# Path attention's preparation: raw products two slabs apart, and root and reciprocal replaced by a power on GpSimd

## The chip, the core and the metric

The kernel runs on one core of a Trainium2 chip. The time is device microseconds (us) of one execution of the whole program. Before the change it is 2883.48 us, the median of three runs (2875.68 to 2893.51). The core's engines work side by side and are tied together by semaphores only: PE (TensorE, matrix products), DVE (VectorE), ACT (ScalarE), POOL (GpSimd) and SP, which issues the DMAs.

## The reference

The program is a six-step model block (cross attention, linear attention, a top-2 mixture of experts, a filtered cross attention, path attention, an expert-choice layer), all in fp32 on x of 16 x 64 x 256. The change touches the first half of the fifth step. Cut to what matters:

```
q, k, v = (h @ m.T for m in (q_w, k_w, v_w))            # h: layer norm of x
w_raw = h @ w1.T @ w2.T                                 # low rank, 32
w_raw = silu(sum(shift(w_raw, i) * conv_w[:, i] for i in range(3)))
Ah, Bh = even and odd halves of w_raw                   # per head and direction, 16 channels each
Wdir = Ah * cos(theta) + Bh * sin(theta)
Wdir = Wdir * rsqrt(sum(Wdir * Wdir, -1) + 1e-06)       # this line is what changes
beta = 2 * sigmoid(h @ bt_w.T + bt_b)
```

## The kernel before, in words

`path_attention` (from L1678) has two blocks with a barrier between them. The first, the **preparation**, makes q, k, v, the directions w and the scaled directions wb for all 1024 tokens. The second, from L1967, solves the triangular systems and the attention batch by batch; it is untouched but for its line numbers. Nothing of the second block starts before every engine has ended the first.

The 512 direction channels are four groups g = 0 to 3 of 128 rows; a group's tile is 128 x 1024 (all tokens), and PSUM takes it in halves of 512 columns. PSUM has 8 banks of 128 x 512: the raw products (and later v) use banks 0 to 3, the norms banks 4 and 5, the projections banks 6 and 7.

- **Raw products** of group g (PE, L1811): four 32 x 512 products, two kinds (a = 0, 1) by two halves. ACT copies each twice out of PSUM (L1854, L1856, the second scaled by the last tap of the convolution) and counts `r_sb`.
- **Slabs** (PE, L1791): twelve projections of 128 output rows, four each for beta, k and q. Each is two halves of two accumulated products; ACT evicts each half (L1864 with the sigmoid, L1866). A slab's half can start only when ACT has evicted the same half of the slab before.
- `convolve(g)` (DVE, L1896, L1898): four instructions. `silu(g)` (ACT, L1839): one over both kinds. `rotate(g)` (DVE, L1904 to L1907): four products and sums, the last of them the square.
- `norms(g)` (PE, L1803): two products with a 0/1 matrix, which add the squares over 16 rows. `roots(g)` (ACT, L1844): Sqrt of the two halves, with 1e-6 as bias.
- `normalise(g)` (DVE): `reciprocal` (L1911), then w times it (L1912), then wb (L1915).
- **Values** (PE, L1820): 64 small products, v for every batch; ACT evicts four banks (L1876).

Each engine runs its own list in the order in which the code issues it; a waiting instruction holds up all that are behind it on its engine. PE: raws(g), three slabs, and norms(g-2) from g = 2 on; then the values, norms(2) and norms(3). ACT follows the same order with silu(g-1) and roots(g-2). DVE: convolve(0), then convolve(g), rotate(g-1) and, from g = 2 on, normalise(g-2); rotate(3), normalise(2), normalise(3). POOL only makes masks in this block (L1734 to L1767). SP loads the weights and then the slabs, the next one as soon as the last but one is in PSUM.

ACT loads a table before a function that the loaded one does not hold: here Sigmoid, Silu and Sqrt each need another, Copy none.

One other place matters for the prediction: in the fourth step POOL already raises a column to the power of -1 (L1267, `tk_total`, one column) and multiplies one (L1271).

Of the kernel before, what the change touches and what calls it, by code (L numbers as in the profile page):

```python
# [13 lines left out]
P = 128  # L14
# [1658 lines left out]
def path_attention(core):  # L1673
# [11 lines left out]
    with ExitStack() as stack:  # L1685
# [14 lines left out]
        with ExitStack() as inner:  # L1700
# [6 lines left out]
            conv, bb = isb("conv", [P, 2, G, 3]), isb("beta_bias", [P, G])  # L1707
            raw, ab = isb("raw", [P, 2, 2, NT]), isb("ab", [P, G, 2, NT])
            blocks = isb("blocks", [P, P])
            eps = isb("eps", [P, 1])  # L1710
            w_loaded, slab_loaded = sem("weights_loaded"), [sem(f"slab_loaded{i}") for i in range(2)]
            step, p_ps, p_sb = sem("step"), sem("proj_in_psum"), sem("proj_ready")
            l_ps, l_sb, r_ps, r_sb = sem("low_in_psum"), sem("low_ready"), sem("raw_in_psum"), sem("raw_ready")
            c_done, s_done, sq_done, n_ps, n_sb, n_used, b_done = (sem(n) for n in ("conv_done", "silu_done", "square_done",
                "norm_in_psum", "norm_ready", "w_ready", "wb_ready"))
            v_ps, v_sb = sem("v_in_psum"), sem("v_ready")
            block = inner.enter_context(nc.Block())
            SLABS = [("beta", wb), ("k", k), ("q", q)]
# [10 lines left out]
            @block.gpsimd  # L1729
            def _(pool):  # L1730
                core.zero_last_stage(pool)
                c = Chain(chained, pool)
                g = nc.gpsimd
                select = lambda o, pattern, base, cm, fill, op=ALU.is_ge: c.link(g.affine_select(  # L1734
                    out=o, in_=o, compare_op=op, fill=fill, base=base, pattern=pattern, channel_multiplier=cm))
                c.step(g.memset(eps[:], 1e-6))
                upper, mincl = mq_mask[:, 0], mq_mask[:, 1]
                for o, value in ((upper, 1.0), (mincl, -1.0), (below[:], 1.0), (causal[:], 0.0), (ident_c[:], 0.0),
                                 (blocks[:], 1.0)):
                    c.link(g.memset(o, value))  # L1740
                halves = (slice(0, T), slice(T, P))
                for rows in halves:
                    select(mq_mask[rows, 0], [[1, T]], -1, -1, 0.0)
                    select(mq_mask[rows, 1], [[1, T]], 0, -1, 0.0)
                    select(below[rows, :], [[-1, T]], -1, 1, 0.0)
                    select(causal[rows, :], [[-1, T]], 0, 1, -1e30)
                    select(ident_c[rows, :], [[-1, T]], 0, 1, 1.0, ALU.not_equal)

                def same_blocks(s, o):

                    c.link(g.memset(o[:], 1.0))
                    for rows in halves:
                        select(o[rows], [[-s, T // s], [0, s]], 0, 1, 0.0)
                        select(o[rows], [[s, T // s], [0, s]], s - 1, -1, 0.0)

                same_blocks(2, same)
                c.link(g.tensor_tensor(firstT[:], same[:], upper, ALU.mult))
                c.link(g.tensor_scalar(firstT[:], firstT[:], -1.0, None, ALU.mult))
                for n, s in enumerate(LEVELS):
                    m = levelT[:, n, :]  # L1760
                    same_blocks(2 * s, m)
                    c.link(g.tensor_tensor(m, m, same[:], ALU.subtract))
                    c.link(g.tensor_tensor(same[:], m, same[:], ALU.add))
                    c.link(g.tensor_tensor(m, m, upper, ALU.mult))
                select(blocks[:], [[-16, P // 16], [0, 16]], 0, 1, 0.0)
                select(blocks[:], [[16, P // 16], [0, 16]], 15, -1, 0.0)
                g.memset(same[:], 0.0).then_inc(masks, 1)  # L1767

            @block.tensor
            def _(pe):  # L1770
                ln.tensor(pe)
                pe.wait_ge(w_loaded, 6 * 16)
                for n in range(2):
                    pe.wait_ge(ln.xnT_ready, 2 * n + 2)
                    for c in range(KD):
                        mm = nc.tensor.matmul(ps[0:32, 4 + n, :], w1[:, c, :], ln.xnT[:, c, n * 512:(n + 1) * 512],
                                              start=(c == 0), stop=(c == KD - 1))
                    mm.then_inc(l_ps, 1)
                pe.wait_ge(l_sb, 2)
                made = 0  # L1780

                def slabs(count):

                    nonlocal made
                    for m in range(made, made + count):
                        pe.wait_ge(slab_loaded[m % 2], 16 * (m // 2 + 1))
                        for n in range(2):
                            if m:
                                pe.wait_ge(p_sb, 2 * (m - 1) + n + 1)
                            for c in range(KD):  # L1790
                                mm = nc.tensor.matmul(ps[:, 6 + n, :], wsm[:, m % 2, c, :],  # L1791
                                                      ln.xnT[:, c, n * 512:(n + 1) * 512], start=(c == 0), stop=(c == KD - 1))
                            mm.then_inc(p_ps, 1)
                    made += count

                def norms(g):

                    pe.wait_ge(masks, 1)
                    pe.wait_ge(sq_done, g + 1)
                    for n in range(2):  # L1800
                        if g:
                            pe.wait_ge(n_sb, 2 * g + n - 1)
                        nc.tensor.matmul(ps[:, 4 + n, :], blocks[:], ab[:, g, 1, n * 512:(n + 1) * 512],  # L1803
                                         start=True, stop=True).then_inc(n_ps, 1)

                for g in range(G):
                    if g:
                        pe.wait_ge(r_sb, 4 * g)
                    for a in range(2):
                        for n in range(2):  # L1810
                            nc.tensor.matmul(ps[:, 2 * a + n, :], w2[:, a, g, :], w32[:, n * 512:(n + 1) * 512],  # L1811
                                             start=True, stop=True).then_inc(r_ps, 1)
                    slabs(3)
                    if g >= 2:
                        norms(g - 2)
                pe.wait_ge(r_sb, 16)
                for b in range(B):
                    for e in range(2):
                        for c in range(KD):
                            mm = nc.tensor.matmul(ps[T * e:T * e + T, b // 4, (b % 4) * P:(b % 4 + 1) * P],  # L1820
                                                  ln.xnT[:, c, b * T:(b + 1) * T], wv[:, c, e, :],
                                                  start=(c == 0), stop=(c == KD - 1))
                    if b % 4 == 3:
                        mm.then_inc(v_ps, 1)
                norms(2)
                norms(3)

            @block.scalar
            def _(act):
# [8 lines left out]
                    act.wait_ge(c_done, 2 * g + 2)  # L1838
                    nc.scalar.activation(ab[:, g], ab[:, g], ACT.Silu, bias=core.zero[:]).then_inc(s_done, 1)  # L1839

                def roots(g):
                    for n in range(2):
                        act.wait_ge(n_ps, 2 * g + n + 1)
                        nc.scalar.activation(ab[:, g, 0, n * 512:(n + 1) * 512], ps[:, 4 + n, :], ACT.Sqrt,  # L1844
                                             bias=eps[:]).then_inc(n_sb, 1)

                for g in range(G):
                    if g >= 2:
                        act.wait_ge(c_done, 2 * g - 2)
                    for a in range(2):  # L1850
                        for n in range(2):
# [3 lines left out]

                            nc.scalar.activation(ab[:, g, a, half], ps[:, 2 * a + n, :], ACT.Copy,  # L1856
                                                 scale=conv[:, a, g, 2:3]).then_inc(r_sb, 1)
                    for _ in range(3):
                        kind, dst = SLABS[m // G]
                        for n in range(2):  # L1860
                            act.wait_ge(p_ps, 2 * m + n + 1)
# [3 lines left out]
                            else:  # L1865
                                nc.scalar.activation(o, ps[:, 6 + n, :], ACT.Copy).then_inc(p_sb, 1)  # L1866
                        m += 1
                    if g:
                        silu(g - 1)
                    if g >= 2:  # L1870
                        roots(g - 2)
                silu(G - 1)
                roots(2)
                for n in range(4):
                    act.wait_ge(v_ps, n + 1)
                    nc.scalar.activation(v2[:, 4 * n:4 * n + 4, :].rearrange("p b c -> p (b c)"), ps[:, n, :],  # L1876
                                         ACT.Copy).then_inc(v_sb, 1)
                roots(3)

            @block.vector  # L1880
            def _(dve):
# [25 lines left out]
                    v.tensor_tensor(ab[:, g, 1, :], wg, wg, ALU.mult).then_inc(sq_done, 1)  # L1907

                def normalise(g):
                    dve.wait_ge(n_sb, 2 * g + 2)  # L1910
                    c.link(v.reciprocal(ab[:, g, 0, :], ab[:, g, 0, :]))  # L1911
                    v.tensor_tensor(w[:, g, :], w[:, g, :], ab[:, g, 0, :], ALU.mult).then_inc(n_used, 1)  # L1912
                    dve.wait_ge(n_used, g + 1)
                    dve.wait_ge(p_sb, 2 * g + 2)
                    v.scalar_tensor_tensor(wb[:, g, :], wb[:, g, :], 2.0, w[:, g, :], ALU.mult, ALU.mult).then_inc(b_done, 1)  # L1915

                convolve(0)
                for g in range(1, G):
                    convolve(g)
                    rotate(g - 1)  # L1920
                    if g >= 2:
                        normalise(g - 2)
                rotate(G - 1)
                normalise(2)
                normalise(3)

# [713 lines left out]
```

## Time and profile before

| what | value |
|---|---|
| median of three runs | 2883.48 us (2875.68 to 2893.51) |
| the profiled execution | 2886.82 us, its span 2885.2 us, so 1.6 us lie around the span |
| PE, DVE, ACT, POOL busy | 85%, 60%, 36%, 25% of the span |
| the preparation | from 1956 to 2075 us of the span, about 119 us |

A row of the timeline gives the start in us, the duration in us, engine, line, operation, the tile written and those read, shapes, and how many instructions were merged; in brackets stands how long the engine idled before it and which engine's instruction ended that. A row of the grouped view gives the busy time in us and the mean in ns.

### The profile page before, as it was taken

The numbers are of one execution on the slowest core, as the hardware profiler recorded it, in microseconds if no ns is written. First come the engines' busy times: TensorE is split into PE (matmuls) and PEld (weight loads), VectorE is DVE, ScalarE is ACT, GpSimd is POOL, SyncE is SP. The second block draws the span as 40 slices with busy tenths as digits, with TensorE's granted clock in tenths as the row PEclk, the third lists the DMA queues.
The fourth block names the chain that finished last, engine by engine and source line by source line (L and its number), as shares of the span: only waits on it lengthen the run. The fifth ranks groups of instructions, "written<-read, shape, count | busy, mean of one in ns | idle before, by whom it ended". The sixth has DMA issues, their size and how long they took to land. (4 is left out here: it accounts for less than half of the span.)

```text
span 2885.2 us, 72779 instructions
## 1 busy us (share of the span) xinstructions
PE 2444.3 (85%) x32208; PEld 1743.3 (60%) x32208; DVE 1741.4 (60%) x2753; ACT 1049.5 (36%) x1558; POOL 719.9 (25%) x735
## 2 busy tenths in 40 slices
PE   5888888898987899988888886787589999998598
PEld 2555555555554455545555554553388888887487
DVE  4565565566654444469999993914866666664500
ACT  2444444444434111145555553024333333332211
POOL 6920000000000000013323324002166666663200
PEclk9999999999998889989999997898799999998699
DMA  2100001001000011222232211001000000000131
GB/s 75 40 21 25 36 21 40 21 21 40 21 2 23 0 34 38 64 83 70 72 102 70 70 53 51 1 0 34 2 4 3 3 4 4 3 4 2 59 146 44
DMA packets 23551, 101.48 MB, mean 35 GB/s; under 512 B 4824, under 2 KB 9837, under 8 KB 16494
## 3 DMA queue, kind: packets, MB, share of 16 engines
q1 hardware_dynamic: 23278, 97.31, 10.5%
q8 instruction: 237, 3.88, 0.6%
q14 instruction: 36, 0.29, 0.0%
HBM read 96.25 MB, written 1.05 MB: 34 GB/s over the span
## 5 line engine op out<-in xcount | busy, mean ns | idle before, releaser
L609 DVE TENSOR_TENSOR xa_probT<-psum,xa_minus_max_spread 128x2048 f32<-128x2048 f32 (+1 forms) x112 | 239.5, 2139 | 167.9 <-PE psum L353 167.5
L592 DVE TENSOR_REDUCE xa_minus_max_parts<-psum 128x4 f32<-128x1600 f32 (+1 forms) x128 | 233.8, 1827 | 166.1 <-PE psum L334 166.1
L522 ACT ACTIVATE xa_probT<-xa_probT,zero_column 128x2048 f32<-128x2048 f32 (+1 forms) x112 | 210.5, 1880 | 271.6 <-DVE xa_probT L609 271.6
L1982 POOL TENSOR_TENSOR pa_cT<-pa_mt_and_minus_qw,pa_levelT 128x512 f32<-128x512 f32 x160 | 200.1, 1273 | 135.4 <-DVE pa_mt_and_minus_qw L2240 125.3
L1264 POOL TENSOR_TENSOR tk_exp_all<-tk_exp_all,tk_exp_left 128x577 f32<-128x577 f32 x64 | 120.9, 1890 | 352.9 <-ACT tk_exp_left L1385 352.9
L2051 PE MATMUL psum<-pa_inv,pa_cT 64*64 64x64 f32 x4096 | 161.6, 234 | 51.5 <-DVE pa_prob L2257 42.6
L2210 ACT ACTIVATE pa_x<-psum 128x256 f32<-128x256 f32 x256 | 98.4, 384 | 287.8 <-PE psum L2051 279.2
L2051 PEld LDWEIGHTS psum<-pa_inv,pa_cT 64*64 64x64 f32 x4096 | 147.4, 147 | 62.6 <-POOL pa_cT L1982 46.2
L701 POOL MEMSET la_v<- 128x512 f32 x1 | 0.5, 525 | 735.2 <-remote 735.2
L334 PE MATMUL psum<-xa_kT,xa_qb 32*128 32x400 f32 (+1 forms) x1024 | 126.9, 566 | 66.2 <-DVE xa_probT L609 45.2
L324 PE MATMUL psum<-xa_wv,xa_ctxT 64*128 64x256 f32 x1248 | 179.6, 395 | 3.3 <-ACT xa_v L515 2.2
L1432 DVE MAX8 tk_top<-tk_left 128x8 f32<-128x1601 f32 x96 | 175.1, 1824 | 4.1
L1434 DVE MATCH_REPLACE8 tk_left<-tk_top,tk_left 128x1601 f32<-128x1601 f32 x96 | 173.9, 1811 | 0.0
L311 PE MATMUL psum<-xa_ctxT,xa_wk 64*128 64x401 f32 (+1 forms) x768 | 170.2, 558 | 3.9 <-ACT xa_kT L506 3.1
L1337 PE MATMUL psum<-tk_ctx,tk_attnT 128*128 128x192 f32 (+1 forms) x832 | 147.8, 336 | 14.7 <-ACT tk_attnT L1391 14.0
L1317 PE MATMUL psum<-tk_ctxT,tk_qwt 97*128 97x512 f32 (+1 forms) x256 | 128.3, 585 | 36.8 <-ACT tk_ctxT L1407 32.6
L2244 DVE STREAM_TRANSPOSE pa_inv<-pa_invT 128x256 f32<-128x256 f32 x256 | 110.2, 440 | 71.4 <-POOL pa_invT L1990 64.8
L324 PEld LDWEIGHTS psum<-xa_wv,xa_ctxT 64*128 64x128 f32 x1248 | 118.0, 182 | 57.8 <-issue 36.6
L1337 PEld LDWEIGHTS psum<-tk_ctx,tk_attnT 128*128 128x128 f32 (+1 forms) x832 | 139.0, 195 | 21.3 <-ACT tk_attnT L1391 21.3
L2287 DVE TENSOR_TENSOR pa_invT<-pa_invT,psum 128x256 f32<-128x256 f32 x256 | 102.4, 400 | 78.0 <-PE psum L2051 75.6
L353 PE MATMUL psum<-xa_qb,xa_kT 32*128 32x128 f32 (+1 forms) x3328 | 128.4, 286 | 21.7 <-DVE xa_minus_max_parts L592 15.4
L2051 PE MATMUL psum<-pa_invT,pa_x 64*64 64x64 f32 x4096 | 140.6, 226 | 1.4 <-issue 1.4
(461 smaller groups left out, 4692.6 us busy)
## 6 DMA issues: line engine op xcount, KB each, us to landing
xa_ctxT<-in_xa_ctx SPq DMA_DIRECT2D x16, 1344.0 KB, 5.8
tk_ctx<-in_ctx SPq DMA_DIRECT2D x16, 1248.0 KB, 5.5
tk_ctxT<-in_ctxT SPq DMA_DIRECT2D x16, 1200.8 KB
ec_w<-in_ec_w SPq DMA_DIRECT2D x16, 1024.0 KB, 6.8
m_gate_up<-in_m_gate_up SPq DMA_DIRECT2D x17, 256.0 KB, 2.6
m_down<-in_m_down SPq DMA_DIRECT2D x17, 128.0 KB, 2.4
ff_w<-in_ff_w SPq DMA_DIRECT2D x2, 1024.0 KB
x_resident<-in_x SPq DMA_DIRECT2D x1, 1024.0 KB, 4.9
```

The costliest lines, as they stand in the source:

```text
L311: mm = mmul(ps[:, 5 + half, 0:z - a], wk[rows, k, m * P:(m + 1) * P], ctxT[rows, h, k, a:z], start=(k == 0), stop=(k == 2))
L324: mm = mmul(ps[0:width(c), 5 + half, i % 2 * D:(i % 2 + 1) * D], ctxT[rows, h, k, at:at + width(c)], wv[rows, k, :], start=(k == 0), stop= ...
L353: mm = mmul(ps[0:w, j, (2 * r + c) * P:(2 * r + c + 1) * P], kT[quad[j], h, r, at:at + w], qb[quad[j], h, r, :, :].rearrange("p e t -> p ( ...
L522: a_(o, o, ACT.Exp, bias=core.zero[0:w]).then_inc(e_done, 1)
L592: v_.tensor_reduce(part[:, :, n // 4, n // 2 % 2 + 2 * (n % 2)], ps[:, 0:4, 0:z - a], AX.X, ALU.max, negate=True).then_inc(m_used, 1)
L609: v_.tensor_tensor(o[:, :, 0:chunks], got[:, :, 0:chunks], shift[0:w, h].rearrange("p j r n -> p (j r) n").unsqueeze(2).broadcast_to([w, 8 ...
L1317: nc.tensor.matmul(flat[:, a:z], qwt[0:CH + 1, g, h, :], ctxT[0:CH + 1, h, 0, a:z], start=True, stop=False)
L1337: mm = nc.tensor.matmul(flat[:, CCOL:CCOL + C], aT[0:width(c), c, :], ctx[0:width(c), h, c, :], start=(c == KC - 1), stop=(c == 7))
L1432: c.step(nc.vector.max(best, src))
L1434: c.step(nc.vector.match_replace(left[:, u % 2, :], best, src, TAKEN))
L1982: g_.tensor_tensor(cT[:, (NL * b + n) % 2, gs], mt_of(b, gs), pair(levelT[:, n, :]), ALU.mult).then_inc(level_ready, 1)
L2051: mm = mmul(ps[rows, bank, column + j * T:column + (j + 1) * T], left[rows, j, :], right[rows, j, :], start=True, stop=True)
```

## The change

The raw products of the groups stand two slabs apart on PE and ACT, not three, and norms(0) to norms(2) stand between the last slabs, ahead of the values. ACT no longer takes a root: `squares(g)` is an Identity that adds 1e-6 and evicts. POOL then raises the 128 x 1024 tile to the power of -1/2 with one instruction per group. On DVE the reciprocal is gone; normalise(g) waits for POOL's `root_ready`, and only normalise(0) stands ahead of rotate(3).

```
-            eps = isb("eps", [P, 1])
+            eps, minus_half = isb("eps", [P, 1]), isb("minus_half", [P, 1])
...
@@ gpsimd, behind the last mask
+                for n in range(G):
+                    pool.wait_ge(n_sb, 2 * n + 2)
+                    g.tensor_tensor(ab[:, n, 0, :], ab[:, n, 0, :], minus_half[:].broadcast_to([P, NT]), ALU.pow
+                                    ).then_inc(root_ready, 1)
@@ tensor
+                for g in range(G):
+                    raws(g)
+                    slabs(2)
+                slabs(1)
+                norms(0)
+                slabs(2)
+                norms(1)
+                slabs(1)
+                norms(2)
                 pe.wait_ge(r_sb, 16)
...
+                values(range(B))
                 norms(3)
@@ scalar
-                        nc.scalar.activation(ab[:, g, 0, n * 512:(n + 1) * 512], ps[:, 4 + n, :], ACT.Sqrt,
+                        nc.scalar.activation(ab[:, g, 0, n * 512:(n + 1) * 512], ps[:, 4 + n, :], ACT.Identity,
                                              bias=eps[:]).then_inc(n_sb, 1)
...
+                raws(0)
+                slabs(2)
+                raws(1)
+                slabs(2)
+                silu(0)
+                raws(2)
+                slabs(2)
+                silu(1)
+                raws(3)
+                slabs(3)
+                silu(2)
+                squares(0)
+                slabs(2)
+                silu(3)
+                squares(1)
+                slabs(1)
+                squares(2)
...
-                roots(3)
+                squares(3)
@@ vector, normalise
-                    dve.wait_ge(n_sb, 2 * g + 2)
-                    c.link(v.reciprocal(ab[:, g, 0, :], ab[:, g, 0, :]))
+                    dve.wait_ge(root_ready, g + 1)
                     v.tensor_tensor(w[:, g, :], w[:, g, :], ab[:, g, 0, :], ALU.mult).then_inc(n_used, 1)
...
-                    if g >= 2:
-                        normalise(g - 2)
+                    if g >= 3:
+                        normalise(g - 3)
                 rotate(G - 1)
-                normalise(2)
-                normalise(3)
+                for g in range(1, G):
+                    normalise(g)
```

On PE, the end of the preparation before, from the third group's raw products on (`pa_w_slab` are the slabs, `pa_w` alone the raw products, `pa_blocks` the norms, `pa_wv` the values):

```order
L1811 MATMUL psum<-pa_w 128x512 x4
L1791 MATMUL psum<-pa_ln_xnT,pa_w_slab 128x512 x12
L1803 MATMUL psum<-pa_ab,pa_blocks 128x512 x2
L1811 MATMUL psum<-pa_w 128x512 x4
L1791 MATMUL psum<-pa_ln_xnT,pa_w_slab 128x512 x12
L1803 MATMUL psum<-pa_ab,pa_blocks 128x512 x2
L1820 MATMUL psum<-pa_wv,pa_ln_xnT 64x128 x64
L1803 MATMUL psum<-pa_ab,pa_blocks 128x512 x4
```

and with the change:

```order
L1818 MATMUL psum<-pa_w 128x512 x4
L1797 MATMUL psum<-pa_ln_xnT,pa_w_slab 128x512 x8
L1818 MATMUL psum<-pa_w 128x512 x4
L1797 MATMUL psum<-pa_ln_xnT,pa_w_slab 128x512 x12
L1809 MATMUL psum<-pa_ab,pa_blocks 128x512 x2
L1797 MATMUL psum<-pa_ln_xnT,pa_w_slab 128x512 x8
L1809 MATMUL psum<-pa_ab,pa_blocks 128x512 x2
L1797 MATMUL psum<-pa_ln_xnT,pa_w_slab 128x512 x4
L1809 MATMUL psum<-pa_ab,pa_blocks 128x512 x2
L1826 MATMUL psum<-pa_wv,pa_ln_xnT 64x128 x64
L1809 MATMUL psum<-pa_ab,pa_blocks 128x512 x2
```

A slab is four matmuls here. The last raw products stand behind six slabs, where they stood behind nine; three norms stand ahead of the values, where one and a half did.

On ACT, the end of the preparation with the change (L1856 is silu, L1861 the eviction of the squares, L1886 that of the slabs, L1908 that of the values):

```order
L1886 ACTIVATE pa_q<-psum 128x512 x2
L1856 ACTIVATE pa_ab<-pa_ab,zero_column 128x2048
L1861 ACTIVATE pa_ab<-psum,pa_eps 128x512 x2
L1886 ACTIVATE pa_q<-psum 128x512 x4
L1856 ACTIVATE pa_ab<-pa_ab,zero_column 128x2048
L1861 ACTIVATE pa_ab<-psum,pa_eps 128x512 x2
L1886 ACTIVATE pa_q<-psum 128x512 x2
L1861 ACTIVATE pa_ab<-psum,pa_eps 128x512 x2
L1908 ACTIVATE pa_v<-psum 128x512 x4
L1861 ACTIVATE pa_ab<-psum,pa_eps 128x512 x2
```

No table load is left among them; before, the whole preparation had seven, six of them for the eight silus and roots; now it has two, for the first sigmoid and the first silu.

On POOL, the end of the preparation and the start of the next block with the change:

```order
L1735 AFFINE_SELECT pa_blocks<-pa_blocks 128x128 x2
L1769 MEMSET pa_same_block 128x64
L1772 TENSOR_TENSOR pa_ab<-pa_ab,pa_minus_half 128x1024 x4
L1700 UNCONDITIONAL_BRANCH
L2001 UNCONDITIONAL_BRANCH
L2006 TENSOR_TENSOR pa_wt<-pa_w,pa_pair_mask 128x512
```

The four powers (L1772) are new and stand behind the masks; nothing but the next block is queued behind them on POOL.

## Rows read from the trace of the kernel before

**Rows 1.** The page's head: span, then busy time and share of each engine.

```profile
span 2885.2 us, 72779 instructions
...
PE 2444.3 (85%) x32208; PEld 1743.3 (60%) x32208; DVE 1741.4 (60%) x2753; ACT 1049.5 (36%) x1558; POOL 719.9 (25%) x735
```

**Rows 2.** Busy time in stretches: length, PE, PEld, DVE, ACT, POOL, clock, DMA.

```profile
1986.00:2045.00 59.00, 57.32 (x238) 27.36 (x236) 40.09 (x28) 42.13 (x57) 0.00 (x0) 0.97 0.07 18
2045.00:2057.00 12.00, 0.20 (x1) 0.23 (x2) 11.86 (x8) 3.42 (x7) 0.00 (x0) 0.69 0.00 0
2057.00:2075.00 18.00, 3.25 (x4) 0.94 (x4) 17.52 (x6) 1.42 (x3) 0.03 (x1) 0.59 0.00 0
```

**Rows 3.** Timeline of DVE at the preparation's end.

```profile
2023.87 6.54 DVE L1911 RECIPROCAL pa_ab<-pa_ab 128x1024 f32<-128x1024 f32 x1
...
2065.59 6.54 DVE L1911 RECIPROCAL pa_ab<-pa_ab 128x1024 f32<-128x1024 f32 x1
2072.17 1.22 DVE L1912 TENSOR_TENSOR pa_w<-pa_w,pa_ab 128x1024 f32<-128x1024 f32 x1
2073.43 1.22 DVE L1915 SCALAR_TENSOR_TENSOR pa_wb<-pa_wb,pa_w 128x1024 f32<-128x1024 f32 x1
```

**Rows 4.** Timeline of POOL behind the barrier.

```profile
2074.97 1.04 POOL L1975 TENSOR_TENSOR pa_wt<-pa_w,pa_pair_mask 128x512 f32<-128x512 f32 x1 [92.08 <-SPq L1961]
```

**Rows 5.** Timeline of PE in the preparation.

```profile
1973.90 12.54 PE L1791 MATMUL psum<-pa_ln_xnT,pa_w_slab 128*128 128x512 f32 x24
1986.37 3.69 PE L1811 MATMUL psum<-pa_w 32*128 32x512 f32 x8
1990.00 10.57 PE L1791 MATMUL psum<-pa_ln_xnT,pa_w_slab 128*128 128x512 f32 x24
...
2009.41 7.10 PE L1791 MATMUL psum<-pa_ln_xnT,pa_w_slab 128*128 128x512 f32 x16 [1.58 <-ACT pa_k L1866]
2016.35 1.88 PE L1803 MATMUL psum<-pa_ab,pa_blocks 128*128 128x512 f32 x4
...
2035.69 7.26 PE L1820 MATMUL psum<-pa_wv,pa_ln_xnT 128*64 128x128 f32 x128
```

**Rows 6.** Timeline of ACT: first and last copies of group 1, a silu, a root.

```profile
1987.53 0.60 ACT L1854 ACTIVATE pa_raw<-psum 128x512 f32<-128x512 f32 x1 [0.36 <-PE psum L1811]
...
1991.17 0.74 ACT L1856 ACTIVATE pa_ab<-psum,pa_conv 128x512 f32<-128x512 f32 x1
...
2001.22 1.28 ACT L1839 ACT_TABLE_LOAD   x1
2002.51 2.00 ACT L1839 ACTIVATE pa_ab<-pa_ab,zero_column 128x2048 f32<-128x2048 f32 x1
...
2020.35 1.26 ACT L1844 ACTIVATE pa_ab<-psum,pa_eps 128x512 f32<-128x512 f32 x2
```

**Rows 7.** Timeline of DVE: the first convolve, its first and last of four.

```profile
1975.22 1.27 DVE L1896 SCALAR_TENSOR_TENSOR pa_ab<-pa_raw,pa_conv,pa_ab 128x1008 f32<-128x1008 f32 x1 [11.00 <-ACT pa_ab L1856]
...
1978.99 1.25 DVE L1898 SCALAR_TENSOR_TENSOR pa_ab<-pa_raw,pa_conv,pa_ab 128x992 f32<-128x992 f32 x1
```

**Rows 8.** Grouped view of DVE: one instruction of a rotate.

```profile
L1907 DVE TENSOR_TENSOR pa_ab<-pa_w 128x1024 f32<-128x1024 f32 x4 | 4.9, 1225 | 0.1
```

**Rows 9.** Grouped view of POOL: the power, a product of one column, larger ones.

```profile
L1264 POOL TENSOR_TENSOR tk_exp_all<-tk_exp_all,tk_exp_left 128x1024 f32<-128x1024 f32 x32 | 75.6, 2362 | 21.1 <-ACT tk_exp_left L1385 21.1
...
L2005 POOL TENSOR_TENSOR pa_prob<-pa_prob,pa_mx 128x1024 f32<-128x1024 f32 x16 | 30.4, 1903 | 48.9 <-DVE pa_mx L2262 48.9
...
L1267 POOL TENSOR_TENSOR tk_total<-tk_total,tk_minus 128x1 f32<-128x1 f32 x32 | 17.9, 560 | 0.0
...
L1271 POOL TENSOR_TENSOR tk_scale<-tk_tile_token_mask,tk_total 128x1 f32<-128x1 f32 x32 | 6.1, 191 | 3.1 <-POOL tk_total L1267 1.1
```

**Rows 10.** Timeline of POOL's masks; the second row lies beside rows 7.

```profile
1973.39 1.15 POOL L1734 TENSOR_SCALAR_AFFINE_SELECT pa_levelT<-pa_levelT 64x64 f32<-64x64 f32 x4
...
1976.95 3.70 POOL L1734 TENSOR_SCALAR_AFFINE_SELECT pa_levelT<-pa_levelT 64x64 f32<-64x64 f32 x4
```

More of the change, by code:

```diff
@@ L1715, in path_attention @@
                 "norm_in_psum", "norm_ready", "w_ready", "wb_ready"))
+            root_ready = sem("root_ready")
             v_ps, v_sb = sem("v_in_psum"), sem("v_ready")
@@ L1736, in _ @@
                 c.step(g.memset(eps[:], 1e-6))
+                c.step(g.memset(minus_half[:], -0.5))
                 upper, mincl = mq_mask[:, 0], mq_mask[:, 1]
@@ L1804, in norms, with raws @@
                                          start=True, stop=True).then_inc(n_ps, 1)
-                for g in range(G):
+                def raws(g):
                     if g:
@@ L1812, in _, with values @@
                                              start=True, stop=True).then_inc(r_ps, 1)
-                    slabs(3)
-                    if g >= 2:
-                        norms(g - 2)
-                pe.wait_ge(r_sb, 16)
[L1817 to L1825, printed above, removed]
+                def values(bs):
+                    for b in bs:
+                        for e in range(2):
+                            for c in range(KD):
+                                mm = nc.tensor.matmul(ps[T * e:T * e + T, b // 4, (b % 4) * P:(b % 4 + 1) * P],
+                                                      ln.xnT[:, c, b * T:(b + 1) * T], wv[:, c, e, :],
+                                                      start=(c == 0), stop=(c == KD - 1))
+                        if b % 4 == 3:
+                            mm.then_inc(v_ps, 1)
+                for g in range(G):
[7 more added lines that the diff above has]
+                norms(2)
+                pe.wait_ge(r_sb, 16)
+                values(range(B))
                 norms(3)
@@ L1839, in silu, with squares, raws @@
                     nc.scalar.activation(ab[:, g], ab[:, g], ACT.Silu, bias=core.zero[:]).then_inc(s_done, 1)
-                def roots(g):
+                def squares(g):
                     for n in range(2):
                         act.wait_ge(n_ps, 2 * g + n + 1)
-                        nc.scalar.activation(ab[:, g, 0, n * 512:(n + 1) * 512], ps[:, 4 + n, :], ACT.Sqrt,
+                        nc.scalar.activation(ab[:, g, 0, n * 512:(n + 1) * 512], ps[:, 4 + n, :], ACT.Identity,
                                              bias=eps[:]).then_inc(n_sb, 1)
-                for g in range(G):
+                def raws(g):
                     if g >= 2:
@@ L1857, in _, with slabs @@
                                                  scale=conv[:, a, g, 2:3]).then_inc(r_sb, 1)
-                    for _ in range(3):
+                def slabs(count):
+                    nonlocal m
+                    for _ in range(count):
                         kind, dst = SLABS[m // G]
@@ L1867, in _ @@
                         m += 1
[L1868 to L1873, printed above, removed]
+                raws(0)
[15 more added lines that the diff above has]
+                squares(2)
                 for n in range(4):
@@ L1920, in _ @@
                     rotate(g - 1)
-                    if g >= 2:
-                        normalise(g - 2)
+                    if g >= 3:
+                        normalise(g - 3)
                 rotate(G - 1)
-                normalise(2)
-                normalise(3)
+                for g in range(1, G):
+                    normalise(g)
         mq, rhs = sb("mt_and_minus_qw", [P, 2, G, 4, 2, T]), sb("rhs", [P, G, 4, T])
```

## The prediction

> **What bounds the kernel now.** The page's head comes first: PE is busy 85% of the span, so a change to DVE, ACT and POOL counts only where PE waits [rows 1]. The view of stretches shows where that is. While PE works without a break (1986 to 2045 us) it is busy 57.3 of 59 us and DVE 40. In the last 30 us of the preparation PE is busy 3.5 us, POOL hardly at all, and DVE 29.4 [rows 2]. So PE bounds the preparation up to about 2045, and DVE its end. The timeline of DVE tells what the end is made of: four reciprocals of 6.54 us, the first at 2023.87 and the last at 2065.59, and behind the last two products; DVE ends at 2074.65 [rows 3]. POOL starts the next block 0.3 us later [rows 4]. Whatever the last engine ends earlier or later moves the rest of the program with it, since the next block is the same; that is the whole of the effect, and its size is "end of the preparation before (2074.65) minus the new end".
>
> **The change part by part.** I walk the new lists with the durations of the trace.
>
> Removed: four reciprocals, 26.2 us of DVE, the last two of which (13.1 us) stand bare at the end [rows 3]; and of ACT's table loads of 1.28 us five [rows 6], which mattered only where DVE or PE waited for ACT.
>
> Moved: raw products two slabs apart. PE takes 3.69 us for a group's raw products and 10.57 / 3 = 3.52 for a slab; the first three slabs are slower, 12.54 / 3 = 4.18 each [rows 5]. Group 0's end stays, 1973.9; slabs 0 and 1 at 2 x 4.18 later, at 1982.3; group 1 at 1986.0; slabs 2 and 3 at 1993.0; group 2 at 1996.7; slabs 4 and 5 at 1996.7 + 7.0 + a wait of 1.6 for ACT, as before [rows 5] = 2005.4; group 3 at 2009.1; slabs 6 to 8 at 2009.1 + 10.6 + about 0.8 for ACT = 2020.5. ACT copies a group in 1991.9 - 1987.5 = 4.4 us, and a silu is 2.0 [rows 6]: silu(1) ends at 2008.1, group 3's copies at 2012.5, and silu(2), behind the eviction of slab 8, at 2023.1. DVE (4 x 1.26 = 5.0 us for a convolve, 4 x 1.22 = 4.9 for a rotate [rows 7, 8]) ends convolve(3) at 2018.0 and rotate(2), which waits for silu(2), at 2028.0. DVE is never late in this part: that cover hides the earlier convolutions, and the two-slab distance alone is worth nothing at the end.
>
> Norms. Two products take 1.88 us [rows 5], the two evictions 1.26 [rows 6]. norms(0) ends at 2022.4, squares(0) behind silu(2) at 2024.4. PE goes on: slabs 9 and 10 to 2029.4, norms(1) to 2031.3, slab 11 to 2034.8, norms(2) to 2036.7, the values (7.26 [rows 5]) to 2044.0, norms(3) to 2045.9. ACT: silu(3) ends at 2032.0, squares(1) at 2033.3, squares(2) at 2037.3, squares(3) at 2046.5. PE's load is the same and its last product ends near where the third norms ended before; all gain lies in the tail.
>
> The tail. POOL's powers can start at 2024.4, 2033.3, 2037.3 and 2046.5, one behind the other, each T long. After the last DVE has two products, 2.5 us [rows 3], and 0.1 for the semaphore. The end is the later of 2046.5 + T and 2024.4 + 4T, plus 2.6. normalise(0) ahead of rotate(3) costs nothing while T is under 12, since PE reads that square only behind the values, at 2044, and 2024.4 + T + 2.6 + 4.9 is earlier.
>
> **T is the unknown.** No row shows a power of 1024 columns. The rows around it: a power of one column takes 0.560 us, a product of one column 0.191, 1024 columns of other arithmetic 1.90 (second operand broadcast, as here) and 2.36 [rows 9]. Low end: all of the excess, 0.560 - 0.191 = 0.37, is set-up, T = 1.90 + 0.37 = 2.3. High end: the excess is paid in every column, T = 0.37 x 1024 + 1.9 = 380. Between them I go by proportion. A product's one column is nearly all set-up (0.191 against 2.36 for 1024), and if the power's splits the same way it keeps the ratio 0.560 / 0.191 = 2.9: T = 2.9 x 2.36 = 6.9. The nearest row of the same work at the same width agrees, the reciprocal with 6.54 [rows 3]. I take **6.9**, and keep both ends for the range. Then the end is 2046.5 + 6.9 + 2.6 = 2056.0 (the other term gives 2054.6), 18.7 us earlier.
>
> The GPSIMD Engine Reference of the Trainium skill (section 3.1) says that in a body of three or more operations per element POOL gets about three operations a cycle, so that extra arithmetic is paid in each column and not as set-up. By its 1.2 GHz my 6.9 us would leave 8 cycles, some 24 operations, to a column, which is an estimate of that page and tight for a power. One column cannot confirm or refute it; it speaks for the first rival below.
>
> Contention. Four mask instructions of POOL take 1.15 us alone and 3.70 beside DVE's first convolve [rows 7, 10], whose instructions read two tiles of SBUF: POOL ran at about a third of its pace. rotate and normalise read two tiles as well. Taken in full, the power of group 0 loses 2.4 us to rotate(2), that of group 1 5 us to normalise(0) and rotate(3), the other two 1.7 us each to a normalise; the chain of four powers becomes 2024.4 + 27.6 + 10.8 + 2.6 = 2065.4, 9.2 us earlier than before. Not at all gives 18.7. A power may touch SBUF less often than a mask does, so I take the middle: **14 us earlier**.
>
> The same page (section 8) states that POOL shares its SBUF interfaces with VectorE and contends with instructions of two SBUF inputs. By that rule at full strength the sum would be -9, by ignoring it -19; the rows show that it exists and not how much a power feels.
>
> Nothing else has a price. The four evictions as Identity last as the roots did; one more memset of 128 x 1 stands ahead of the masks, but POOL has nothing left to do from 1986 on [rows 2], and its first power is due at 2024; SP's slab loads wait on PE as before. Sum against the profiled execution: 2886.8 - 14 = 2872.8. That execution stands 3.3 us above the median, so against the median 2883.5 - 14 = **2870**.
>
> **The rivals.**
>
> - *Powers on the path, slower than before.* The price is the chain 2024.4 + 4T + 2.6: it passes 2074.65 at T = 11.9 without contention, 9.2 with it, and the kernel then loses 4 us for each us of T. At T = 19 it is 29 us slower, at 30 (the geometric middle of the two ends) 72 us: 2956; at 60, 192 us: 3076; at the high end over 4300. For it: an operation made of a logarithm and an exponential should cost per column, and 11.6 ns a column are enough, of the 370 that one column showed. Against it: the ratio above, and the reciprocal. The rule of section 3.1 named above is this rival's.
> - *The full low end.* T = 2.3, no contention: 2046.5 + 2.3 + 2.6 = 2051.4, a gain of 23: 2860. It cannot be much more, since even T = 0 leaves 26.
> - *The gain does not come.* T near 10, or PE's list a few us longer because ACT holds up slabs: 2880 to 2890. Nothing in the rows puts PE later than 2050, so this is T again.
>
> **How the numbers follow.** About 1% (29 us) is what a measurement of this kernel can tell from no change. T below about 10, a gain of up to 23 us: 0.42. T of 10 to about 17 or 19, from no change to 29 us slower: 0.10. Something that cancels the gain for another reason: 0.02. T above that: 0.44, of which 0.27 lies below T = 60. Over 29 us faster would need more than the tail has: 0.02. So within 1% is 0.54, slower 0.44, faster 0.02. The range reaches from the low end with the scatter of the runs (2860 - 4) to T near 60 (3080), and leaves out 0.17 above and a little below. The first case's own range is 2856 to 2884. As cases of both signs hold most of the chance, the predicted time is that of the first, 2870, not a mean.
>
> **What would show it.** In the profile after: the power's four rows. Around 7 us each, DVE idle between rotate(3) and the last normalise in pieces of 2 to 6 us, and POOL's first instruction of the next block near 2061: right. Powers longer than 12 us, back to back, with DVE waiting for POOL on each `root_ready`: the first rival. Powers that last longer where DVE runs a rotate: contention. PE's last norms after 2050, or table loads among the squares, would make the walk wrong. ACT should show two table loads between the layer norm and the barrier.

## The result, and the profile after

The changed kernel takes **3495.93 us** (median of four runs, 3483.77 to 3497.68) against 2882.11 before: the ratio is 1.2115, its 95% interval 1.2068 to 1.2163. It is 614 us slower. Forecast were 2870 us and a range up to 3080.

The page's head and its costliest groups tell it at once. Of its two costliest groups the first was not in the kernel before:

```profile
span 3482.2 us, 72775 instructions
...
PE 2435.7 (70%) x32208; PEld 1736.2 (50%) x32208; DVE 2046.4 (59%) x2749; ACT 1043.1 (30%) x1553; POOL 1372.7 (39%) x740
...
L1772 POOL TENSOR_TENSOR pa_ab<-pa_ab,pa_minus_half 128x1024 f32<-128x1024 f32 x4 | 653.9, 163479 | 45.1 <-ACT pa_ab L1861 45.1
L1943 DVE TENSOR_TENSOR pa_w<-pa_w,pa_ab 128x1024 f32<-128x1024 f32 x4 | 251.3, 62814 | 309.6 <-POOL pa_ab L1772 309.6
```

A power of 128 x 1024 takes **163.5 us** on POOL, where the prediction put 6.9. POOL's busy time rose by 652.8 us [rows 1], which is the four powers. The second line is a product on DVE that took 1.22 us before [rows 3] and now has a mean of 62.8; that is told below.

The stretches of the changed kernel, as [rows 2] are those of before (length; PE, PEld, DVE, ACT, POOL busy; clock; DMA):

```profile
1950.00:2022.00 72.00, 64.68 (x138) 26.87 (x139) 38.38 (x55) 42.45 (x65) 21.56 (x69) 0.84 0.11 34
2022.00:2676.00 654.00, 24.87 (x159) 13.93 (x157) 344.17 (x14) 11.11 (x17) 653.50 (x4) 0.52 0.00 0
```

POOL is busy in all of the 654 us, PE in 25 of them, at a granted clock of 0.52, which is nearly all the lower level, 1.2 GHz. DVE's end, with the last power in front of it, and the start of the next block, which answer to [rows 3] and [rows 4]:

```profile
2512.35 83.33 DVE L1943 TENSOR_TENSOR pa_w<-pa_w,pa_ab 128x1024 f32<-128x1024 f32 x1 [78.59 <-POOL pa_ab L1772]
2595.72 1.23 DVE L1946 SCALAR_TENSOR_TENSOR pa_wb<-pa_wb,pa_w 128x1024 f32<-128x1024 f32 x1
2675.53 1.23 DVE L1943 TENSOR_TENSOR pa_w<-pa_w,pa_ab 128x1024 f32<-128x1024 f32 x1 [78.59 <-POOL pa_ab L1772]
2676.79 1.23 DVE L1946 SCALAR_TENSOR_TENSOR pa_wb<-pa_wb,pa_w 128x1024 f32<-128x1024 f32 x1
```

```profile
2021.64 164.28 POOL L1772 TENSOR_TENSOR pa_ab<-pa_ab,pa_minus_half 128x1024 f32<-128x1024 f32 x1 [45.05 <-ACT pa_ab L1861]
...
2678.33 1.04 POOL L2006 TENSOR_TENSOR pa_wt<-pa_w,pa_pair_mask 128x512 f32<-128x512 f32 x1 [2.83 <-SPq L1992]
```

The powers run from 2021.64 without a gap to 2675.5; then come DVE's 2.5 us and the next block. To compare kernels I use the **stage**, from DVE's first statistics of this layer norm to POOL's first product of the next block. It is 2074.97 - 1956.16 = 118.8 us before and 2678.33 - 1949.95 = 728.4 after. The two starts (1956.16 and 1949.95) are those rows of the two timelines:

```profile
1956.16 2.71 DVE L146 BATCH_NORM_STATS2 pa_ln_stats<-x_resident 128x6 f32<-128x256 f32 x8 [0.54 <-PEq L1644]
```

```profile
1949.95 2.71 DVE L146 BATCH_NORM_STATS2 pa_ln_stats<-x_resident 128x6 f32<-128x256 f32 x8 [0.54 <-PEq L1644]
```

The stage is 609.6 us longer, the median time 614. The spans of the two profiled executions differ by 597.0 us only: outside the stage the one with the change is 12.6 us shorter, 6.2 ahead of the stage and 6.4 behind it, at a granted clock 0.01 higher in both parts. That is within the scatter of the runs (14 us between the four of the changed kernel), so the stage is where the loss lies.

### The profile page after: what moved, and what is told of

Same layout as the page of the kernel before. It is cut to its first block and busy times, and to the rows that moved or that the text cites. A ratio compares the mean times of both kernels' runs of the same rounds, so it can differ in the third digit from the quotient of the medians.

```text
span 3482.2 us, 72775 instructions
## 1 busy us (share of the span) xinstructions
PE 2435.7 (70%) x32208; PEld 1736.2 (50%) x32208; DVE 2046.4 (59%) x2749; ACT 1043.1 (30%) x1553; POOL 1372.7 (39%) x740
## 5 line engine op out<-in xcount | busy, mean ns | idle before, releaser
L1772 POOL TENSOR_TENSOR pa_ab<-pa_ab,pa_minus_half 128x1024 f32<-128x1024 f32 x4 | 653.9, 163479 | 45.1 <-ACT pa_ab L1861 45.1
L1943 DVE TENSOR_TENSOR pa_w<-pa_w,pa_ab 128x1024 f32<-128x1024 f32 x4 | 251.3, 62814 | 309.6 <-POOL pa_ab L1772 309.6
L2096 PE MATMUL psum<-pa_moving,pa_wt 32*128 32x128 f32 x512 | 19.7, 292 | 400.3 <-POOL pa_wt L2006 400.3
L2096 PEld LDWEIGHTS psum<-pa_moving,pa_wt 32*128 32x128 f32 x512 | 16.6, 194 | 402.9 <-ACT pa_moving L2218 401.8
L1809 PE MATMUL psum<-pa_ab,pa_blocks 128*128 128x512 f32 x16 | 11.3, 843 | 232.3 <-issue 232.3
L2275 DVE STREAM_TRANSPOSE pa_inv<-pa_invT 128x256 f32<-128x256 f32 x256 | 110.2, 440 | 71.7 <-POOL pa_invT L2021 65.0
```

What stands on the lines that cost most here:

```text
L1772: g.tensor_tensor(ab[:, n, 0, :], ab[:, n, 0, :], minus_half[:].broadcast_to([P, NT]), ALU.pow).then_inc(root_ready, 1)
```

## The experiments

The theory (A) is that POOL pays for a power in every column, and that the chain of four powers is the whole loss. The rivals are that the new order costs part of it (B), that the wait for POOL or the broadcast operand is what costs, and that DVE and POOL hold each other up so that the powers come out long (B1).

**The order alone.** Root on ACT and reciprocal on DVE as before, in the changed kernel's order:

```
-                for n in range(G):
-                    pool.wait_ge(n_sb, 2 * n + 2)
-                    g.tensor_tensor(ab[:, n, 0, :], ab[:, n, 0, :], minus_half[:].broadcast_to([P, NT]), ALU.pow
-                                    ).then_inc(root_ready, 1)
...
-                        nc.scalar.activation(ab[:, g, 0, n * 512:(n + 1) * 512], ps[:, 4 + n, :], ACT.Identity,
+                        nc.scalar.activation(ab[:, g, 0, n * 512:(n + 1) * 512], ps[:, 4 + n, :], ACT.Sqrt,
...
-                    dve.wait_ge(root_ready, g + 1)
+                    dve.wait_ge(n_sb, 2 * g + 2)
+                    c.link(v.reciprocal(ab[:, g, 0, :], ab[:, g, 0, :]))
```

> The order of the changed kernel with the root on ACT and the reciprocal on DVE as before; POOL makes no power. Theory A (all of the loss is the four powers on POOL, one behind the other): about the time of before. By the walk of lists DVE ends rotate(2) about 118.5 - 46.6 = 72 us after the stage's start and then has 9.0 + 4.9 + 3 x 9.0 = 40.9 us of work, so the stage takes about 113 us in place of 118.5: 2877 us, ratio 0.998. Rival B (the order, by holding PE's norms behind DVE, costs a good part of the 610 us): far above 2900.

Measured: 2885.97 us against 2883.33, ratio 1.0005 (0.9986 to 1.0025); the stage is 116.4 us. With root and reciprocal the order costs nothing, and B falls as the cause of the 610 us. It gains 2.4 us of stage, not the 5.5 expected, because rotate(2) ends 75.4 us after the start and not 71.9: its first instruction waits for ACT, as in the row

```profile
2026.41 1.22 DVE L1932 TENSOR_TENSOR pa_w<-pa_ab,filter_rotary 128x1024 f32<-128x1024 f32 x1 [7.66 <-ACT pa_ab L1852]
```

where the stage began at 1955.90. (Two norms stood ahead of the values before, norms(0) and norms(1), and not one and a half as the section on the change has it.)

**The power alone**, in the order of before (the same edit the other way round, on the kernel before).

> The order of the kernel before, with only the root and the reciprocal replaced by POOL's power. Theory A: the four powers of 163.4 us follow each other from the end of the first eviction of squares (2021.6 in the trace of before) and DVE needs 2.5 us more: the stage ends at 2677.8 and takes 721.6 us, the kernel 3486, as bad as the whole change. Rival B (the new order made it bad): well under 3400.

Measured, one execution: 3489.62 us, stage 721.1 us, against 721.6 expected. The row of POOL, whose four powers are merged, and of the next block:

```profile
2023.53 653.87 POOL L1772 TENSOR_TENSOR pa_ab<-pa_ab,pa_minus_half 128x1024 f32<-128x1024 f32 x4 [37.80 <-ACT pa_ab L1850]
2680.22 1.04 POOL L1980 TENSOR_TENSOR pa_wt<-pa_w,pa_pair_mask 128x512 f32<-128x512 f32 x1 [2.82 <-SPq L1966]
```

The power alone makes the stage 721.1 - 118.8 = 602.3 us longer, of the 609.6 of the whole change. The other 7.3 us go to the new order once powers are in it: on PE it puts norms(0) behind one group's raw products more (4.46 us there), so the first power starts 71.7 us after the stage's start (2021.64 - 1949.95) and not 64.4 (2023.53 - 1959.10), and the chain of four moves with its start. The size of this part is less sure than that of the first: in another run of the changed order (the one called "what is held" below) the first power starts after 68.5 us.

**Powers of four widths.**

```
+                    cols = (1, 128, 512, 768)[n]
-                    g.tensor_tensor(ab[:, n, 0, :], ab[:, n, 0, :], minus_half[:].broadcast_to([P, NT]), ALU.pow
+                    g.tensor_tensor(ab[:, n, 0, 0:cols], ab[:, n, 0, 0:cols], minus_half[:].broadcast_to([P, cols]), ALU.pow
...
-                    v.scalar_tensor_tensor(wb[:, g, :], wb[:, g, :], 2.0, w[:, g, :], ALU.mult, ALU.mult).then_inc(b_done, 1)
+                    v.scalar_tensor_tensor(wb[:, g, :], wb[:, g, :], 0.0, w[:, g, :], ALU.mult, ALU.mult).then_inc(b_done, 1)
```

> The changed kernel with powers of 1, 128, 512 and 768 columns in place of four of 1024; wb is multiplied by 0.0, so beta is left out of the result. Theory A, paid in every column: 0.4 us + 0.159 us per column, so 0.56, 20.8, 82 and 123 us, and a kernel about 427 us shorter than the changed one (3065). Rival, a price per instruction or per block of 1024 columns: the four are nearly equal, or 512 and 768 not in proportion. DVE's product that starts as the next power starts: if it is held for half of the power, about 41 us beside the 512 and 61 beside the 768; if it is held until 512 columns are left, 0 and 41.

Measured, one execution: 3073.18 us. The grouped view of POOL, shapes kept apart, and two rows of DVE, the products that start beside the power of 512 and beside that of 768 columns:

```profile
L1773 POOL TENSOR_TENSOR pa_ab<-pa_ab,pa_minus_half 128x768 f32<-128x768 f32 x1 | 122.6, 122626 | 0.0
L1773 POOL TENSOR_TENSOR pa_ab<-pa_ab,pa_minus_half 128x512 f32<-128x512 f32 x1 | 81.9, 81921 | 0.0
L1773 POOL TENSOR_TENSOR pa_ab<-pa_ab,pa_minus_half 128x128 f32<-128x128 f32 x1 | 21.8, 21759 | 7.0 <-ACT pa_ab L1862 7.0
L1773 POOL TENSOR_TENSOR pa_ab<-pa_ab,pa_minus_half 128x1 f32<-128x1 f32 x1 | 1.6, 1571 | 45.1 <-ACT pa_ab L1862 45.1
```

```profile
2060.13 2.06 DVE L1944 TENSOR_TENSOR pa_w<-pa_w,pa_ab 128x1024 f32<-128x1024 f32 x1 [18.04 <-POOL pa_ab L1773]
...
2142.02 82.91 DVE L1944 TENSOR_TENSOR pa_w<-pa_w,pa_ab 128x1024 f32<-128x1024 f32 x1 [78.58 <-POOL pa_ab L1773]
```

From 512 to 768 columns (122.63 - 81.92) / 256 = **0.159 us a column**; the straight line through both has 0.5 us at no column, and meets the 163.2 us of 1024. The first two each started within 0.1 us of a DVE product (at 2029.69 and 2038.27) and are about 1 us longer than this line for that. So the price is paid in each column, and the 0.560 us of the one-column row [rows 9] was 0.16 of column and 0.4 of set-up. On the second question both guesses were wrong for 768 columns: DVE's product lasts 82.9 us beside them and 83.3 beside 1024, that is about as long as the first 512 columns are made (512 x 0.159 = 81.4). Beside 512 it lasts 2.06 us, only 0.8 more than its 1.22.

**A product in place of the power**, of the same shape and operands:

```
-                    g.tensor_tensor(ab[:, n, 0, :], ab[:, n, 0, :], minus_half[:].broadcast_to([P, NT]), ALU.pow
+                    g.tensor_tensor(ab[:, n, 0, :], ab[:, n, 0, :], minus_half[:].broadcast_to([P, NT]), ALU.mult
...
-                c.step(g.memset(minus_half[:], -0.5))
+                c.step(g.memset(minus_half[:], 1e-3))
```

> The changed kernel with POOL's power replaced by a product with 0.001 of the same shape and operands; the normalisation is left out of the result. Theory A: POOL's instruction takes 1.9 to 2.4 us, the broadcast operand costs nothing, and the stage ends where the walk of the prediction put it for its low end: about 23 us ahead of before, 2860, ratio 0.992, some 3 us more if DVE's products hold POOL up. Rival: the broadcast second operand or the wait for POOL is what costs, then the instruction stays far above 2.4 us, or the gain stays under 10 us.

Measured: 2865.8 us, ratio 0.9933 (0.9905 to 0.9961); stage 98.0 us, 20.8 less than before. POOL and DVE where the first two products meet a rotate:

```profile
2028.95 2.90 POOL L1772 TENSOR_TENSOR pa_ab<-pa_ab,pa_minus_half 128x1024 f32<-128x1024 f32 x1 [45.01 <-ACT pa_ab L1861]
2037.53 1.95 POOL L1772 TENSOR_TENSOR pa_ab<-pa_ab,pa_minus_half 128x1024 f32<-128x1024 f32 x1 [5.67 <-ACT pa_ab L1861]
```

```profile
2028.88 1.22 DVE L1937 TENSOR_TENSOR pa_ab<-pa_ab,filter_rotary 128x1024 f32<-128x1024 f32 x1
2030.13 2.80 DVE L1938 TENSOR_TENSOR pa_w<-pa_w,pa_ab 128x1024 f32<-128x1024 f32 x1
...
2037.64 2.91 DVE L1937 TENSOR_TENSOR pa_ab<-pa_ab,filter_rotary 128x1024 f32<-128x1024 f32 x1
```

The broadcast operand and the hand-over to POOL cost next to nothing: 1.95 and 2.90 us for the two shown, a mean of 2.22 over four. The walk's low end (23.3 us earlier) holds to 2.5 us. Contention works both ways: POOL's first is 1.0 us long because DVE was ahead, DVE's two are 1.6 and 1.7 us longer than 1.22 because POOL was.

**Halves**: each power cut into two of 512 columns.

```
+                    for h in range(2):
+                        half = slice(h * 512, h * 512 + 512)
+                        ins_ = g.tensor_tensor(ab[:, n, 0, half], ab[:, n, 0, half], minus_half[:].broadcast_to([P, 512]), ALU.pow)
+                    ins_.then_inc(root_ready, 1)
```

> The changed kernel with each power cut into two of 512 columns. The run with narrower powers held DVE's product for 82.9 us beside 768 columns and hardly beside 512. Theory A1 (a power of over 512 columns holds DVE's reads of two tiles while its first 512 are made, and the chain of powers alone sets the end): no DVE instruction lasts over 3 us, norms(2) follows at once, yet the kernel takes as long as the changed one, 3484 to 3497. Rival B1 (holding and being held lengthens the powers): eight halves of less than 81.6 us, and a kernel tens of us shorter.

Measured, one execution: 3502.41 us, stage 730.7 us. POOL's line and three of DVE's two-tile instructions:

```profile
L1774 POOL TENSOR_TENSOR pa_ab<-pa_ab,pa_minus_half x8: 81911/81912/82967, 2034.7 to 2609.0; 128x512 f32<-128x512 f32 x8
```

```profile
2035.88 1.95 DVE L1940 TENSOR_TENSOR pa_w<-pa_w,pa_ab 128x1024 f32<-128x1024 f32 x1
...
2199.60 2.06 DVE L1945 TENSOR_TENSOR pa_w<-pa_w,pa_ab 128x1024 f32<-128x1024 f32 x1 [160.51 <-POOL pa_ab L1774]
```

No DVE instruction beside the powers lasts longer than 2.06 us, and the halves still take 81.9: the 251 us that DVE's products seemed to cost were beside the chain, not in it. B1 falls. This is how to read a busy DVE at 62.8 us a product (three of 83.3 and one of 1.2): it is a wait that the profile shows as work.

**What is held.** More DVE work beside the third and the fourth power:

```
+                    if g == 1:
+                        dve.wait_ge(p_sb, 24)
+                        c.link(v.tensor_copy(raw[:, 0, 1, :], raw[:, 0, 0, :]))
+                        c.link(v.tensor_tensor(raw[:, 0, 0, 0:512], raw[:, 0, 1, 0:512], ps[:, 6, :], ALU.add))
+                        c.link(v.tensor_tensor(raw[:, 0, 0, 0:64], raw[:, 0, 1, 0:64], raw[:, 1, 0, 0:64], ALU.add))
+                    if g == 2:
+                        c.link(v.tensor_scalar(raw[:, 0, 1, :], raw[:, 0, 0, :], 2.0, None, ALU.mult))
```

> The changed kernel with more DVE work beside two powers of 1024 columns: as the third power starts a copy of 1024 columns, a sum of a SBUF and a PSUM tile (512 columns), and a sum of two SBUF tiles (64 columns), then normalise; as the fourth starts a product of one tile with a number, then normalise. Theory: only what reads two SBUF tiles is held, so the copy, the sum with PSUM and the product with a number take about 1.2 us or less, and the sum of 64 columns over 75 us. Rival: everything that reads SBUF is held, then the copy takes 83 us. Either way the kernel's time stays near 3490.

Measured, one execution: 3486.67 us. First POOL's line (shortest, median and longest in ns; start of the first and of the last), then its row from the second power on, in which three are merged, then DVE's rows. The third power runs from about 2348.3 to the start of the fourth at 2511.5; the fourth ends at 2185.15 + 490.02 = 2675.2.

```profile
L1772 POOL TENSOR_TENSOR pa_ab<-pa_ab,pa_minus_half x4: 163205/163432/164279, 2020.9 to 2511.5; 128x1024 f32<-128x1024 f32 x4
```

```profile
2185.15 490.02 POOL L1772 TENSOR_TENSOR pa_ab<-pa_ab,pa_minus_half 128x1024 f32<-128x1024 f32 x3
```

```profile
2348.41 163.70 DVE L1945 COPY pa_raw<-pa_raw 128x1024 f32<-128x1024 f32 x1 [73.81 <-POOL pa_ab L1772]
2512.15 0.69 DVE L1946 TENSOR_TENSOR pa_raw<-pa_raw,psum 128x512 f32<-128x512 f32 x1
2512.87 81.49 DVE L1947 TENSOR_TENSOR pa_raw<-pa_raw 128x64 f32<-128x64 f32 x1
2594.40 1.22 DVE L1950 TENSOR_TENSOR pa_w<-pa_w,pa_ab 128x1024 f32<-128x1024 f32 x1
2595.66 1.22 DVE L1953 SCALAR_TENSOR_TENSOR pa_wb<-pa_wb,pa_w 128x1024 f32<-128x1024 f32 x1
2596.80 78.93 DVE L1949 TENSOR_SCALAR pa_raw<-pa_raw 128x1024 f32<-128x1024 f32 x1
```

My theory fell for the copy. There are three classes. The sum with PSUM is not held (0.69 us). What reads two SBUF tiles is held through the first 512 columns (81.49 us for only 64 columns of work) and not after (1.22). The copy and the product with a number, which read one SBUF tile and write SBUF, are held until the power has ended: the copy for a whole one, the product from 2596.80 to 2675.73, in the half where the others run freely; each ends about 0.6 us behind its power.

"The first 512 columns" is a rule for the power alone. Beside POOL's product of 1024 columns, DVE is held for 1.7 of its 1.95 us, which is more than half. One reading fits all these rows, an estimate that no row shows directly: what holds DVE's second SBUF tile is POOL taking in its operands, 512 columns at a time, at 0.84 us for 512 (2.06 - 1.22 beside 512 columns); the second part is taken in when the first has been worked off. By it the hold should be 0.42 us longer beside 1024 columns than beside 768, and 83.33 - 82.91 is 0.42. Why the copy and the product with a number wait for the end it does not say.

**Logarithm and exponential on ACT.** The gain of the order can be had if neither DVE nor POOL makes the power. In short (`logs(g)` is `squares(g)` with ACT.Ln; PE waits for it in place of n_sb, and DVE runs all four normalise behind rotate(3)):

```
+                def power(g, from_psum):
+                    if not from_psum:
+                        act.wait_ge(n_sb, 2 * g + 2)
+                        nc.scalar.activation(ab[:, g, 0, :], ab[:, g, 0, :], ACT.Ln, bias=core.zero[:]).then_inc(log_ready, 2)
+                    act.wait_ge(log_ready, 2 * g + 2)
+                    nc.scalar.activation(ab[:, g, 0, :], ab[:, g, 0, :], ACT.Exp, bias=core.zero[:], scale=-0.5
+                                         ).then_inc(root_ready, 1)
...
-                squares(1)
+                power(0, False)
+                logs(1)
+                power(1, True)
...
-                squares(3)
+                logs(3)
+                power(3, True)
```

> The order of the changed kernel, the power made on ACT as exp(-0.5 ln x): logarithm and exponential of 1.1 to 1.3 us each, seven or eight more table loads of 1.28. No reciprocal, nothing on POOL. Theory A: the stage ends about 18 us ahead of before (norms(2) on PE wait for ACT's logarithm of group 1, the last exponential ends near 2053.5 in the time of before, plus 2.5 for DVE): 2864, ratio 0.9935. Rival: ACT becomes the bound with its table loads and holds up slab 11 and the values: no gain.

Measured: 2869.82 us against 2883.33, ratio **0.9946** (0.9924 to 0.9967), stage 106.0 us, 12.8 less than before. ACT does carry more: the last logarithm waits for v's evictions and both table loads lie bare at the end.

```profile
2050.69 0.60 ACT L1923 ACTIVATE pa_v<-psum 128x512 f32<-128x512 f32 x1 [1.05 <-PE psum L1824]
2051.30 1.28 ACT L1867 ACT_TABLE_LOAD   x1
2052.60 1.26 ACT L1867 ACTIVATE pa_ab<-psum,pa_eps 128x512 f32<-128x512 f32 x2
2053.88 1.28 ACT L1861 ACT_TABLE_LOAD   x1
2055.18 1.15 ACT L1861 ACTIVATE pa_ab<-pa_ab,zero_column 128x1024 f32<-128x1024 f32 x1
```

So the rival there was half right: the gain is 12.8 us of stage and not 18. Between every logarithm and exponential stands a table load, eight in all.

**The same, paired.** One logarithm for groups 0 and 1, norms(3) and logs(3) moved ahead, v evicted last:

```
                 squares(1)
+                logs_of_two()
+                power(0)
+                power(1)
                 slabs(1)
+                logs(2)
+                logs(3)
+                power(2)
+                power(3)
...
-                values(range(B))
+                values(range(12))
                 norms(3)
+                values(range(12, B))
```

> As the version with logarithm and exponential on ACT, but one logarithm for groups 0 and 1, logs(2) and logs(3) together, four table loads at the end in place of eight, norms(3) behind three quarters of the values, and v evicted last. Theory A: DVE's last product ends 5 us earlier than in that version, a stage of about 101 us against 106.0 there and 118.8 before: ratio 0.9935 or lower. Rival: the eviction of v or PE's last values now end last, a stage of 104 us or more, no better than that version.

Measured: 2868.93 us against 2882.48, ratio **0.9946** (0.9923 to 0.9969), stage 2061.50 - 1960.93 = 100.6 us. The stage came out as expected, 5.4 us shorter than in the version before it; the ratio cannot show that, since 5 us are 0.2% and the interval is 0.5% wide. Both versions are about half a per cent faster than the kernel before, a small gain that their intervals clear (1 lies outside both), and some 18% faster than the changed one.

## Why the prediction was wrong

- **What bounds the kernel** was right: the effect is the stage's end, 609.6 of the 614 us.
- **The failed step** is the size of one term of the sum, the value of T: "If the power's splits the same way it keeps the ratio 0.560 / 0.191 = 2.9: T = 2.9 x 2.36 = 6.9". The power does not split as a product does. T measured 163.2 us, 24 times that, 0.159 us in each column and about 0.4 in set-up. A product pays 2 ns a column; what an instruction does inside a column cannot be read from a row of one column, and multiplying by a ratio assumed that it could. The agreement with the reciprocal's 6.54 was chance, on another engine.
- **The bounds** held: 163 lies between 2.3 and 380. I took T = 60 as the edge of the range with no row behind it, and so cut off most of the interval between the bounds; the high bound itself was the better guide, within a factor of 2.3. Of the low bound, "all of the excess is set-up", the runs show the opposite: set-up is 0.4 to 0.5 us of 163.
- **The formula of the first rival** was right. 2024.4 + 4 x 163.2 + 2.6 = 2679.8 makes the stage 605 us longer; measured 609.6. The remainder is the walk, 3.5 us late (the first power started 71.7 us after the stage's start and not 68.2), and 1.1 us of contention in the first power.
- **The rule of section 3.1** of the GPSIMD Engine Reference (the Trainium skill), that arithmetic beyond two operations is paid in each column, was set down as a sentence and given no weight in T. The widths bear it out in kind: 0.159 us a column. By the page's 1.2 GHz that is 191 cycles, an estimate of that page's clock.
- **The walk** of the lists was right to a few us: with a cheap instruction on POOL the stage was 20.8 us shorter, where it gave 23.3. The table loads went as said. In the changed kernel slab 8 ends 3.6 us later than in the walk. Of that, 1.7 arose in slabs 6 to 8 behind ACT's copies of group 3 (13.15 us on PE, put at 11.4), 0.7 in group 3's raw products and 1.0 in the first two slabs.
- **Contention** was put at up to 10.8 us in the chain. It cost the chain 1.1 us (the first power, 164.28 against 163.2) and made four DVE instructions 83.3 us long, off the path. That POOL can hold DVE was not among the prediction's terms, which had only POOL slowed by DVE.
- **The chances**: 0.54 within 1% against 0.44 slower put even odds on an unknown of two powers of ten, where any T above 19 us meant slower. By the bounds alone, 2.3 and 380, 96% of the interval lay there if it is counted evenly in us, and 59% if evenly by factors; the ratio and the reciprocal's 6.54 pulled the odds down, and neither was evidence about the power's columns.

## What to carry to other kernels

Before an operation goes from one column to a thousand, time it at two widths; one row at one column gives set-up and price mixed, and only the slope counts. Where a new instruction's price is unknown by a factor of a hundred, work out its break-even first (here 12 us, 12 ns a column) and ask which of the bounds that lies next to. For a power on a wide tile, ACT's logarithm and exponential, 1.15 us each for 1024 columns and 1.28 for a table load, are far cheaper than POOL's power, and in an order that suits them made this stage 18.2 us shorter than root and reciprocal did in the order of before, and 15.8 shorter than in the changed order.

## What the runs showed of the hardware

- POOL's power in fp32 takes 0.159 us a column on 128 partitions, 73 times its product of the same shape (163.2 us against a mean of 2.22). One exponent, -1/2, was measured at these widths.
- While it runs, DVE instructions of one SBUF source and an SBUF target (copy, product with a number) stand still until it ends (163.70 and 78.93 us); those of two SBUF tiles stand still while the first 512 columns of a wider power are made (they last 81.5 to 83.4 us, and 2.06 beside a power of only 512 columns); a sum with PSUM does not (0.69 us). The profile shows the standing as busy time. The GPSIMD Engine Reference of the Trainium skill (section 8) states contention with DVE instructions "in a 2-port perf mode or with two SBUF inputs"; these rows agree for two inputs, and show how long it can last. Whether the copy is held because of such a mode, no run here tells. Why 512 columns are the limit stays open as well; the reading given above for it is an estimate.
- PE's granted clock in the 654 us of powers was 0.52, nearly all of it at the lower of its two levels.
